# Second attention in pairs of key tiles, and a third pair of output buffers in its queries

## The reference

```python
def _L1_xattn_ref(hidden_states, encoder_hidden_states, Wq, Wk, Wv, Wo, gq, gk):
    ...
    q = (hidden_states @ Wq).reshape(B, Sq, H, D)          # H = 16, D = 128
    k = (encoder_hidden_states @ Wk).reshape(B, Skv, H, D)
    v = (encoder_hidden_states @ Wv).reshape(B, Skv, H, D)
    q = rmsnorm(q, gq)
    k = rmsnorm(k, gk)
    scores = jnp.einsum('bqhd,bkhd->bhqk', q, k) * scale
    attn = jax.nn.softmax(scores, axis=-1)
    out = jnp.einsum('bhqk,bkhd->bqhd', attn, v)
    out = out.reshape(B, Sq, H * D)
    return out @ Wo
```

## Time and profile before

| | |
|---|---|
| median of 3 runs | 2333.1 us (2330.64 to 2334.74) |
| profiled execution, its own time | 2329.33 us |
| its span | 2327.6 us |
| queries of the second attention | from about 1466 to 1571 us |
| second attention | from 1571 to 2195 us |
| from there to the end | 132 us |
| PE, DVE, ACT, POOL busy over the span | 90%, 73%, 53%, 53% |

### The profile page before, as it was taken

How to read it: one execution, slowest core, us unless ns; L and a number is a source line. 1 busy time by engine, 2 the same in 40 slices (tenths; PEclk the granted TensorE clock), 3 DMA queues, 4 the chain that set the end, 5 groups by cost and what they waited for, 6 DMA issues and landing times. The chain is left out here.

```text
span 2327.6 us, 46500 instructions
## 1 busy us (share of the span) xinstructions
PE 2092.5 (90%) x16696; PEld 1690.0 (73%) x16696; DVE 1704.9 (73%) x2327; ACT 1230.5 (53%) x2243; POOL 1233.7 (53%) x995
## 2 busy tenths in 40 slices
PE   4899999999999569999999786778999999999875
PEld 2688788788788347777777633557999999999643
DVE  5788888888888566666666333758899999999366
ACT  1688888888888315555555212574444444444302
POOL 1566666666666223443343032353898988989200
PEclk8999999999999769999999868899999999999987
DMA  3524323323332412343332053484223323221400
GB/s 91 157 95 161 120 98 147 118 112 138 117 124 112 164 51 94 142 145 118 116 116 86 16 205 92 117 206 159 107 86 110 119 80 111 84 106 43 176 11 16
DMA packets 115908, 259.92 MB, mean 112 GB/s; under 512 B 48001, under 2 KB 85538, under 8 KB 106642
## 3 DMA queue, kind: packets, MB, share of 16 engines
q1 hardware_dynamic: 111938, 246.79, 30.4%
q10 hardware_dynamic: 2304, 7.34, 0.8%
q0 software_dynamic: 1536, 3.94, 0.5%
HBM read 153.71 MB, written 108.28 MB: 113 GB/s over the span
## 5 line engine op out<-in xcount | busy, mean ns | idle before, releaser
L350 DVE TENSOR_REDUCE rk<-n_sq 128x1024 f32 (+2 forms) x384 | 466.0, 1214 | 120.9 <-ACT n_sq L298 117.5
L298 ACT ACTIVATE n_sq<-n_slot 128x1024 f32<-128x1024 f32 (+1 forms) x384 | 394.2, 1027 | 141.1 <-PE n_slot L258 131.7
L256 PE MATMUL n_slot<-n_wh,n_yh 128*128 128x512 f32 (+1 forms) x768 | 317.8, 414 | 9.5 <-PEq L444 9.5
L1665 ACT ACTIVATE a_pr<-a_sc 128x448 f32<-128x448 f32 (+1 forms) x384 | 204.9, 544 | 191.3 <-PE a_sc L1596 178.9
L1729 DVE TENSOR_REDUCE a_mpart<-a_pre 112x2 f32<-112x1024 f32 (+1 forms) x192 | 218.8, 1184 | 118.3 <-PE a_pre L1567 118.3
L258 PE MATMUL n_slot<-n_wh,n_yl 128*128 128x512 f32 (+1 forms) x768 | 303.3, 395 | 0.0
L257 PE MATMUL n_slot<-n_wl,n_yh 128*128 128x512 f32 (+1 forms) x768 | 302.0, 393 | 0.0
L1368 POOL TENSOR_TENSOR p_S<-p_S,a_mb 128x896 f32<-128x896 f32 x94 | 255.2, 2751 | 69.3 <-ACT a_mb L1413 69.3
L1368 POOL TENSOR_TENSOR a_S<-a_S,a_mb 128x896 f32<-128x896 f32 (+1 forms) x89 | 240.7, 2740 | 39.2 <-ACT a_mb L1413 39.2
L230 POOL TENSOR_TENSOR n_khat<-n_kb,n_rs 128x240 f32<-128x240 f32 x192 | 114.3, 595 | 233.8 <-DVE n_rs L365 233.7
L1426 ACT ACTIVATE p_S<-p_S 128x896 f32<-128x896 f32 x96 | 91.5, 953 | 161.7 <-POOL p_S L1368 158.4
(11 more groups left out here) (361 smaller groups left out, 4665.7 us busy)
## 6 DMA issues: line engine op xcount, KB each, us to landing
vdram<-n_v SPq DMA_DIRECT2D x16, 1632.0 KB, 5.3
a_v<-vdram SPq DMA_DIRECT2D x16, 1632.0 KB, 6.9
kTdram<-n_kT SPq DMA_DIRECT2D x16, 1484.0 KB, 5.0
a_kT<-kTdram SPq DMA_DIRECT2D x16, 1484.0 KB, 7.5
n_yT<-in_ctxT SPq DMA_DIRECT2D x16, 750.0 KB, 8.6
yhdram<-n_yh SPq DMA_DIRECT2D x16, 750.0 KB, 6.4
yldram<-n_yl SPq DMA_DIRECT2D x16, 750.0 KB, 8.6
a_yh<-yhdram SPq DMA_DIRECT2D x16, 750.0 KB, 4.2
```

The costliest lines, as they stand in the source:

```text
L256: pe.matmul(dst, high, wh[:, cols], start=True, stop=False)
L298: act.activation(sq[0:n, w, :], slot[w][0:n, :], ACT.Square).then_inc(slot_free, 1)
L350: dve.tensor_reduce(g.rk[0:n, b, j, 8 * s:8 * s + 8], sq[0:n, (2 * j + s) % 3, :].rearrange("p (h d) -> p h d", h=8), X, ALU.add)\
L1665: act.activation(pr[0:n, s % 4, unit, :], sc[(2 * s + unit) % 3][0:n, 0:HALF], ACT.Exp).then_inc(p_ready, 1)
```

## The change

**Pairs.** On PE, scores(j) and scores(j+1) stand together at even j, in front of the output of j; outputs of tiles keep their j, so that two outputs stand in a row. On DVE, the four units of two tiles stand together, then the two maxima. **Spread.** It moves from j = 2 to j = 3 on PE, and the two banks that it takes from the ring move with it (SLOT). **Normalise.** On DVE it moves from in front of j = 5 to in front of j = 6, behind the maximum of tile 5. **Weights.** In step 1 the products of output and value weights move from j = 3 to j = 2, and ACT copies them ahead of the diagonal blocks. **Queries.** Group 6 takes a third pair of buffers, which lies in `g.xnT` and `xh`, and group 7 buffer 0; from group 5 on DVE makes one half of the low part and POOL the other. **Barrier.** SP's wait for the last stored output moves from the end of the attention to the start of the projection, in front of the load of sequences 8 to 15.

```diff
+    SPREAD = 3
+    SLOT = 2 * SPREAD + 2
+    slot_of = lambda unit: unit + (2 if unit >= SLOT else 0)
...
-    WEIGHTS = {0: (0, 2), 3: (2, 4), 4: (4, 6), 5: (6, NM)}
+    WEIGHTS = {0: (0, 2), 2: (2, 4), 4: (4, 6), 5: (6, NM)}
...
                 for j in range(NK):
-                    if front:
+                    if front and j % 2 == 0:
                         scores(j)
+                        scores(j + 1)
...
-                    if back and j == 2:
+                    if back and j == SPREAD:
                         spread()
...
+            def scaled(b, i, j):
+                n, first = rows(j), isinstance(b, int) and b == 0
+                if from_(b, 2):
+                    dve.wait_ge(p_used, NK * (b - 2) + j + 1)
+                for half in range(1 if first and j in ACT_HALF else 2):
+                    r = (USES * i + slot_of(2 * j + half)) % RING
+                    dve.wait_ge(s_ready, SC * b + 2 * j + half + 1)
+                    ...
+                        rk.unsqueeze(2).broadcast_to([n, 8, NQ]), ALU.mult).then_inc(s_scaled, 1)
...
+                    if end and j == LAG + 1:
+
+                        dve.wait_ge(p_used, NK * (b - 1))
+                        if from_(b, 3):
+                            dve.wait_ge(oT_ready, 2 * (b - 2))
+                        normalise(b)
...
-                    if end and j == LAG:
-                        ...
-                        normalise(b)
-                    if front:
-                        ...
+                    if front and j % 2 == 0:
+                        scaled(b, i, j)
+                        scaled(b, i, j + 1)
                     if back and j == 1:
                         reduced(b, 0)
...
+        qo = [sb(f"qo{i}", [P, B, 2 * NQ])[:, :, :] for i in range(2)] + [by_batch(g.xnT[:, :, :])]
+        qe = [sb(f"qe{i}", [P, B, 2 * NQ], F32R)[:, :, :] for i in range(2)] + [by_batch(xh[:, :, :])]
+        place = [0, 1, 0, 1, 0, 1, 2, 0]
...
-                if v % 4 == 0 and n >= 2:
-                    act.wait_ge(g.q_stored[n % 2], 32 * (n // 2))
+                if v % 4 == 0 and n >= 2 and place[n] < 2:
+                    act.wait_ge(g.q_stored[place[n]], 32 * place[:n].count(place[n]))
...
+            def low_outputs(n):
+                dve.wait_ge(copied, 8 * n + 8)
+                dve.tensor_tensor(qo[place[n]][:, batches(1), :].bitcast(F32R), qo[place[n]][:, batches(1), :],
+                                  qe[place[n]][:, batches(1), :], ALU.subtract).then_inc(dve_lowered, 1)
...
-            sp.wait_ge(stored, 16 * B)
...
         @block.sync
         def _(sp):
+            sp.wait_ge(g.o_stored, 16 * B)
             sp.dma_start(ot[1][:, :, :], g.odram[NB:B].rearrange("b c n -> c b n")).then_inc(ot_in[1], 16)
```

More of the change, by code:

```diff
@@ L776, in phase_queries1 @@
     TR, HL, BACK = 2, 3, NT + 3
+    STORED = [0, 1, 0, 1, 0, 1, 1, 0]
+    SHARED = 5
     with ExitStack() as ctx:
@@ L849, in low_outputs @@
                 pool.wait_ge(q0_split, n + 1)
-                for half in range(2):
-                    batches = slice(B // 2 * half, B // 2 * (half + 1))
+                for half in range(1 if n >= SHARED else 2):
                     pool.wait_ge(copied, 8 * n + 6 + 2 * half)
-                    pool.tensor_tensor(qo[n % 2][:, batches, :].bitcast(F32R), qo[n % 2][:, batches, :], qe[n % 2][:, batches, :],
-                                       ALU.subtract).then_inc(lowered, 1)
+                    pool.tensor_tensor(qo[place[n]][:, batches(half), :].bitcast(F32R), qo[place[n]][:, batches(half), :],
+                                       qe[place[n]][:, batches(half), :], ALU.subtract).then_inc(lowered[half], 1)
             key_weights_of(0)
@@ L1164, in scores @@
                                 pe.wait_ge(s_scaled, SC * b - 3 + use)
-                        elif use in (10, 11):
-                            if from_(b, 1):
-                                pe.wait_ge(mb_ready, 2 * (b - 1) + use - 9)
+                        elif use in (SLOT + 4, SLOT + 5) and not first:
+                            pe.wait_ge(mb_ready, 2 * (b - 1) + use - SLOT - 3)
                         else:
-                            unit = use - 4 if use < 10 else use - 6
+                            unit = use - 4 if use < SLOT + 4 else use - 8 if use < SLOT + 6 else use - 6
                             if first and unit % 2 and unit // 2 in ACT_HALF:
@@ L1214, in spread @@
                         if front:
-                            pe.wait_ge(s_scaled, SC * b + half + 3)
-                        pe.matmul(ring[(USES * i + 6 + half) % RING][:, 0:HALF], ones[:, :],
+                            pe.wait_ge(s_scaled, SC * b + SLOT - 4 + half + 1)
+                        pe.matmul(ring[(USES * i + SLOT + half) % RING][:, 0:HALF], ones[:, :],
                                   diag[:, half * HALF:(half + 1) * HALF], start=True, stop=True).then_inc(mb_psum, 1)
@@ L1401, in step @@
                     weights(*WEIGHTS[0])
+                    weights(*WEIGHTS[2])
                 if back:
@@ L1416, in step @@
                     n = rows(j)
-                    if joined and j + 3 in WEIGHTS:
-                        weights(*WEIGHTS[j + 3])
+                    if joined and j in (0, 1):
+                        weights(*WEIGHTS[j + 4])
                     if back:
```

55 lines of the change are left out of this document (27 added, 28 removed).

## The result

| | before | changed |
|---|---|---|
| median | 2332.98 us (2330.64 to 2334.74, 4 runs) | 2376.95 us (2374.69 to 2377.17, 3 runs) |
| profiled execution, its own time | 2329.33 us | 2377.17 us |
| its span | 2327.6 us | 2375.4 us |

The ratio is 1.0184 (95% interval 1.0169 to 1.0198): 44 us slower. The forecast was 2402 (69 slower), with a range from 2345 to 2420. Direction and range held; the size was too large by 25 us, and the part of the range that belonged to the forecast itself, 2385 to 2420, was missed. A fourth execution of the changed kernel, of 3758.36 us at a granted clock of 0.748, is left out as a slow one.

What follows compares the result with a forecast made beforehand. The prediction took the ring of POOL's shifts, ACT, PE's spread and POOL again as the bound, not PE. Steps 71 + step 1 1.5 - queries 2.5 - barrier 1 = 69, giving 2398, or 2402 as median; range 2345 to 2420.

Steps and rivals of the forecast that it cites:

- The ring before: Second attention, kernel before: POOL's shifts, ACT's last exponential, blocks and copies, and PE's spread set the 36.73 us step.
- A second maximum costs a whole shift: DVE pairs: POOL gets a whole shift between two maxima, 0.86 + 2.06 + 0.86; the second takes 2.9 us.
- Rival 2: DVE's second maximum follows its first at once; step about 36.2 us, 2324 us in all; chance 0.10.
- The ties: Maxima of tiles 8 and 10 nearly tie with POOL's shifts; POOL goes first in both, step 41.8 us.
- The steps' term: Second attention: 5.0 us more in each of 13 whole steps, 3 each in two partial ones, 71 in all.
- the mixed case: Of the two near ties between DVE and POOL, one goes each way: 39.9 us per step, 2376; chance 0.13.
- rival 1: DVE wins both near ties, PE sets the pace from the normalise: step 38.1 us, 2351 in all; chance 0.21.
- What stands behind the last maximum: End of a step: transposes, reduction, tiles 2 and 3, two outputs and two spreads, from 32.73 to 41.8 us.
- The clock: PE's longer waits may drop its granted clock to 1.2 GHz: at most 1 to 2 us per step, up to 20.
- Both are needed: PE's 2.4 us wait for the normalise needs both the pair and the normalise's later place.
- The signs: In a step: second maxima 2.9 us, PE waits about 2.4 and 3.4, POOL idle about 11, cast at last landing.
- Step 1: Weight products copied ahead of the diagonal blocks delay POOL's first shifts some 4 us; 1.5 us lost overall.

Runs made afterwards that it cites:

- e8: Kernel before, with ACT's diagonal blocks and copies to a_mb moved ahead of the last exponential from step 2 on: 2321.44 us, ratio 0.9951.
- e1: Changed kernel, with DVE again taking units and maximum of one tile after the other: 2331.74 us, ratio 0.9998.
- e6: Changed kernel, with a 128x128 memset on DVE added ahead of the maximum of tile 10: 2381.3 us, ratio 1.0207.
- e10: Changed kernel, with DVE's two units of tile 11 run over 128 rows instead of 92: 2404.36 us, ratio 1.0309.
- e2: Changed kernel, with the normalise moved between the maxima of tiles 4 and 5: 2380.18 us, ratio 1.0204.
- e5: Changed kernel, with 12 more matmuls on PE, never read, ahead of its wait for the normalise: 2375.78 us, ratio 1.0184.
- e3: Kernel before, with the normalise alone moved from in front of tile 5's units to in front of tile 6's: 2389.96 us, ratio 1.0234.
- e7: Kernel before, with only the queries and barrier edits of the changed kernel: 2328.83 us, ratio 0.998.

## Why the prediction was right, and where it was not

- **The ring before**: right. e8 took 0.9 us of ACT out of it and gained 0.6 per step.
- **A second maximum costs a whole shift**: right. 2.9 in each pair that meets POOL's shifts, and e1 gives all of the time back. Rival 2, which would have made the kernel faster, is out. This also bears out the Trainium skill (page "SBUF — State Buffer", section "Who interferes with whom") on the port pair that is locked for whole instructions: the loser waits, 2.9 us for a maximum of 0.9 here, and POOL's held shift 2.93 to 2.97.
- **The ties**: this is the step that failed. "I take it that POOL goes first" was right for tile 8 and wrong for tile 10. It stood on the distance of the starts, 0.12 us between 0.07 and 0.21; e6 and e10 show that this distance alone does not decide: tile 10 comes behind units of 92 rows. One turn won takes the last maximum one shift ahead, from 31.6 us behind POOL's first shift (32.73 - 1.13 in the forecast) to 29.8. Where tile 10 is made to lose (e10), the time is 2404 and the steps are mostly 41.9: the forecast's case, 2402 and 41.8. The steps' term was put at 71 us; measured from POOL's first shift of step 1 to that of step 16 it is 596.45 - 552.60 = 43.9 (72.9 in e10).
- **The price of the mixed case**: met within 1 us, in part by luck. 39.9 and 2376 lie midway between the forecast (41.8, 2402) and rival 1 (38.1, 2351), whose step was set by PE; no walk of this case stands behind them. By the turns alone it is 41.8 less one shift of 2.06, 39.7.
- **What stands behind the last maximum**: right. In the forecast, 32.7 to 41.8 (its own terms add up to 41.7); measured 8.9 us from its end to the second spread.
- **Rival 1's price**: the ring was drawn through the normalise and PE. e2 and e5 show that this leg had slack in the changed kernel.
- **The clock**: it fell behind the wait in eight of the loop's twelve steps (0.52 to 0.70) and cost nothing there: the four steps without the fall are as long, and so are those of e5. In e10 it fell behind PE's wait for the last maximum in four steps, and those were 0.9 longer.
- **"Both are needed"**: wrong (e3), with no weight in the sum.
- **The signs**: the second maxima of 2.9 us, PE's wait of 2.6 and the cast at the last landing (1578.71 and 1578.70) came. POOL's idle time of 8.3 lies between the 11 of the forecast and the 6 of rival 1, and the wait of 3.4 ahead of the maxima did not come: it is under 1 us in the loop.
- **Step 1**: 1.5 forecast; from the queries' start to POOL's first shift 144.3 us instead of 142.7, so 1.7. In e1, with the same edit but single tiles on DVE, the first shift comes 4.1 later (146.8), and the steps give 3.7 of it back (548.9 against 552.6 from step 1 to 16), as the prediction pictured displaced work.
- **Queries**: 2.5 gained by forecast, none in the profiled executions of e7 and of the changed kernel. There the lower bound of 1 was too high: the wait moved from ACT to SP's issue and the start of the attention.
- **Barrier**: 1 forecast, 1.0 in e7 and 1.4 here.
- **Sum**: 43.9 + 1.7 - 1.4 = 44.2, the medians' 44.0. The profiled executions differ by 47.8, because the changed one began the queries 3.3 us later (1469.31 against 1466.04), in stages without an edit.

## What to carry to other kernels

In this kernel two engines that take turns at the memory by whole instructions form a grid: a short operation of the one should meet one long operation of the other, and two short ones in a row pay for a long one in between. On such a grid an earlier start is worth nothing until it wins a turn, and one turn moves every step by a whole instruction. When two rings fit a profile, take the wait out of one: filling PE's wait (e5) and moving the normalise (e2) ended an argument that one step of the trace left open. And look at all steps: in four of twelve the clock had not fallen, and they were no shorter.

## What the runs showed of the hardware that was not expected

- Who gets the next turn is not read off the start times alone. In the fourteen traces there are 326 maxima that start within 0.32 us of one of POOL's shifts. Where the units ahead had 128 rows, DVE lost all 204 that started 0.09 to 0.28 us behind POOL and won 33 of the 34 that started earlier or at most 0.01 behind. Where they had 92 rows, it won all 88, at 0.12 to 0.29 us behind. The rows were all that e10 changed.
- After waits of PE of the same 2.6 us the granted clock fell in eight steps and not in four.
- SP's issue of a store is itself drawn out while two earlier stores are under way: 3.34 us where it took 0.37. In the changed kernel the issues begun at 1563.23, 1565.96 and 1569.70 end at 1565.91, 1569.61 and 1573.05, and the stores two ahead of them landed at 1565.26, 1569.21 and 1573.12. Why is not shown. Work that is no longer held back by one wait is then held by the next one in line.
